# Token records of 132 words instead of 258, and the residual row formed again from them on ScalarE

## What is computed

```python
x = x + tanh(g_xattn) * attention(layernorm(x), ctx, ctx)       # 16 heads of 8
x = x + tanh(g_ffn) * moe(layernorm(x))

# moe: T = 4096 tokens, E = 8 experts, capacity C = T / E = 512
gates = softmax(tokens @ Wg); idx = argmax(gates)
place = position of the token among those of its expert (in order); dropped if place >= C
out = gate * (relu(token @ W1[idx] + b1[idx]) @ W2[idx] + b2[idx])    # 0 if dropped
```

## Time and profile before

| | us |
|---|---|
| median of 3 runs | 298.25 |
| lowest and highest | 296.54 and 298.52 |
| profiled execution, its own time | 298.6 |
| its span in the profile | 296.5 |
| attention stage in that span | 0 to some 218 |
| experts' stage | some 218 to the end |

### The profile page before, as it was taken

One profiled execution on the slowest core, in us unless ns is written; L12 is line 12 of the kernel. 1 busy time (PEld: TensorE's weight loads), 2 busy tenths in 40 slices (PEclk: granted clock), 3 DMA queues, 4 the chain that ended last, 5 costly groups with the idle time before them and its releaser, 6 DMA issues.

```text
span 296.5 us, 8184 instructions
## 1 busy us (share of the span) xinstructions
PE 244.5 (82%) x2907; PEld 163.5 (55%) x2907; DVE 196.6 (66%) x663; ACT 155.6 (52%) x375; POOL 182.3 (61%) x246
## 2 busy tenths in 40 slices
PE   1748758788979989999899989995869999999950
PEld 1325525465755755765656666663324677777740
DVE  4676717647978999989897999965302545555440
ACT  5553727567778787787887756681202322222100
POOL 6625916911982998897897968448720056555781
PEclk9998959969999999999999999999595999999995
DMA  4652771990482652661733541138352256554310
GB/s 120 184 162 73 214 217 32 237 293 19 113 235 57 174 158 71 195 182 46 213 110 90 152 126 57 58 102 174 138 144 66 71 170 188 173 180 132 103 55 16
DMA packets 50920, 39.27 MB, mean 132 GB/s; under 512 B 9698, under 2 KB 47223, under 8 KB 50880
## 3 DMA queue, kind: packets, MB, share of 16 engines
q1 hardware_dynamic: 47168, 28.67, 35.9%
q0 software_dynamic: 3712, 10.07, 10.4%
HBM read 13.72 MB, written 12.65 MB: 89 GB/s over the span
## 4 chain that ended last, share of the span: by engine, by line
PE 39%; DVE 13%; DMA 13%; SPq 10%; issue 9%; ACT 8%; POOL 4%; POOLq 0%; ACTq 0%; DVEq 0%
PE X L634 9%; DMA qp<-mrow 8%; DVE negm L833 6%; SPq L347 6%; PE TS L618 5%; PE M L546 3%; ACT prob L703 3%; PE O L513 3%; PE TS L497 3%; PE O L618 3%; PE M L618 2%; PE S L482 2%; PE X L441 2%; SPq L358 2%; POOL rec_dram L1224 2%
## 5 line engine op out<-in xcount | busy, mean ns | idle before, releaser
L703 ACT ACTIVATE prob<-TS 128x512 f32<-128x512 f32 x128 | 72.0, 589 | 40.1 <-PE TS L497 39.2
L833 DVE TENSOR_REDUCE negm<-S 128x4 f32<-128x512 f32 x128 | 81.6, 679 | 8.5 <-PE S L482 7.9
L513 PE MATMUL O<-prob,vals 128*32 128x128 f32 x1024 | 42.1, 283 | 0.8 <-ACT oraw L712 0.8
L1313 POOL DMA_INDIRECT out_dram<-fin,tok x32 | 31.5, 986 | 14.2 <-issue 12.2
L1224 POOL DMA_INDIRECT rec_dram<-rec,slot x32 | 32.2, 1005 | 8.0 <-issue 5.5
L497 PE MATMUL TS<-qp,kp 64*128 64x128 bf16 x512 | 28.1, 221 | 9.7 <-DMA qp<-mrow 9.6
L482 PE MATMUL S<-kp,qp 62*128 62x128 bf16 x512 | 31.3, 222 | 2.3 <-DVE negm L833 2.0
L513 PEld LDWEIGHTS O<-prob,vals 128*32 128x32 f32 x1024 | 24.6, 110 | 13.9 <-ACT prob L703 7.0
L267 POOL TENSOR_TENSOR rest_k<-full_k,parts_k 128x512 f32<-128x512 f32 x7 | 8.0, 1149 | 39.3 <-ACT parts_k L674 39.3
L804 ACT ACTIVATE qp<-TS,b_act 128x512 f32<-128x512 f32 x16 | 11.0, 687 | 39.9 <-PE TS L618 39.9
L634 PE MATMUL X<-w2s,qp 128*128 128x128 f32 x240 | 28.2, 275 | 0.9 <-issue 0.9
(11 more groups left out here) (170 smaller groups left out, 486.8 us busy)
## 6 DMA issues: line engine op xcount, KB each, us to landing
kp<-parts_k SPq DMA_DIRECT2D x48, 128.0 KB, 2.5
qp<-parts_q SPq DMA_DIRECT2D x48, 128.0 KB, 4.1
rec_dram<-zeros POOLq DMA_DIRECT2D x8, 516.0 KB, 6.2
xr<-rec_dram SPq DMA_DIRECT2D x8, 260.0 KB, 3.9
x_sb<-in_x_dram SPq DMA_DIRECT2D x8, 256.0 KB, 3.6
c_sb<-in_ctx_dram SPq DMA_DIRECT2D x8, 256.0 KB, 3.5
out_dram<-rec SPq DMA_DIRECT2D x8, 256.0 KB, 3.3
w1s<-in_L_ffn_W_dram SPq DMA_DIRECT2D x8, 256.0 KB, 4.1
```

The lines of the kernel that those rows point to most:

```text
L513: mm = nc.tensor.matmul(o_out[i * HV:(i + 1) * HV, u * L:(u + 1) * L], vals[G % 2][:, k, h, :], prob[n % 2][:, h * L:(h + 1) * L], start=( ...
L703: nc.scalar.activation(prob[n % 2][:, first:first + 4 * L], TS[:, a, :], ACT.Exp).then_inc(a_exp, 1)
L833: V.tensor_reduce(negm[n % 2][:, first:first + 4], S[:, a, :].rearrange("p (h k) -> p h k", k=L), AX.X, ALU.max, negate=True).then_inc(v_r ...
L1313: G_.indirect_dma_start(out_rows, bass.IndirectOffsetOnAxis(tok[p][:, t:t + 1], 0), fin[p][:, t, :], None, bounds_check=T - 1, oob_is_err= ...
```

## The change

A record now has 132 words: gate, code, mean, deviation sqrt(var + eps), and the normalised row. The row x itself is no longer in it. In SBUF `rec` holds, for each token, x (0 to 127), the eight logits, mean, deviation and the normalised row; gate and code overwrite the last two logits when these have been used, so that a record is one piece of 132 words. In the experts' stage ScalarE forms x again as normalised * deviation + mean, straight into `fin` (`rows_again`), and VectorE adds gate * b2 in place. The rows of expert e-1 are formed in ScalarE's part for expert e. `xr` and its DMAs are gone; `xe`, `gate2`, `tok` and `fin` have three buffers. One small GpSimd operation a group (`deviation`) is new, and `residual2` of the last expert stands earlier. The fill with zeros and the scatters of records keep their number and place; they carry 132 words a record.

```diff
-REC = 2 * P + 2
+REC = P + 4
...
+    GATE, CODE, MEAN, DEV, NORMED = DE - 2, DE - 1, DE, DE + 1, DE + 2
...
-        rec = [sb(f"rec{i}", [P, GB, D + DE]) for i in range(3)]
+        rec = [sb(f"rec{i}", [P, GB, NORMED + D]) for i in range(3)]
...
             def load_xe(e):
 
-                sp.dma_start(xe[e % 2][:], rec_v[e][:, :, 0:D]).then_inc(xe_in[e % 2], 16)
-
-            def load_xr(e):
-
-                sp.dma_start(xr[e % 2][:], rec_v[e][:, :, D:REC]).then_inc(xr_in[e % 2], 16)
+                sp.dma_start(xe[e % 3][:], rec_v[e]).then_inc(xe_in[e % 3], 16)
...
-            for e in range(2):
+            for e in range(3):
                 load_xe(e)
-            for e in range(2):
-                load_xr(e)
-            sp.wait_ge(p_eT, 1)
-            load_xe(2)
 
             for e in range(2, E):
                 sp.wait_ge(p_H, 4 * (e - 1))
                 load_w1(e)
                 if e < E - 1:
-                    sp.wait_ge(p_eT, e)
+                    sp.wait_ge(p_eT, e - 1)
+                    sp.wait_ge(v_code, e - 1)
+                    sp.wait_ge(a_res, e - 1)
                     load_xe(e + 1)
                 sp.wait_ge(p_Y, 2 * (e - 1))
                 load_w2(e)
-                sp.wait_ge(v_res, e - 1)
-                load_xr(e)
...
+            def rows_again(e):
+
+                act.wait_ge(xe_in[e % 3], 16 * (e // 3) + 16)
+                if e >= 3:
+                    act.wait_ge(fin_out[e % 3], 64 * (e // 3))
+                for t in range(ET):
+                    mm = nc.scalar.activation(fin[e % 3][:, t, :], xe[e % 3][:, t, 4:], ACT.Identity,
+                                              bias=xe[e % 3][:, t, 2:3], scale=xe[e % 3][:, t, 3:4])
+                mm.then_inc(a_res, 1)
...
                 nc.scalar.activation(xeT[p][:], S[:, p, :], ACT.Copy).then_inc(a_eT, 1)
+                if e >= 1:
+                    rows_again(e - 1)
+                if e == E - 1:
+                    rows_again(e)
...
             def residual2(e):
 
-                p = e % 2
-                dve.wait_ge(xr_in[p], 16 * (e // 2) + 16)
-                if e >= 2:
-                    dve.wait_ge(fin_out[p], 64 * (e // 2))
...
+                p = e % 3
+                dve.wait_ge(xe_in[p], 16 * (e // 3) + 16)
+                if e >= 3:
+                    dve.wait_ge(fin_out[p], 64 * (e // 3))
...
                 dve.wait_ge(v_gate2, e + 1)
+                dve.wait_ge(a_res, e + 1)
                 for t in range(ET):
                     mm = V.scalar_tensor_tensor(fin[p][:, t, :], b2_all[:, e, :], gate2[p][:, t:t + 1],
-                                                xr[p][:, t, 0:D], ALU.mult, ALU.add)
+                                                fin[p][:, t, :], ALU.mult, ALU.add)
...
             finish(E - 2, 0)
+            residual2(E - 1)
             finish(E - 2, 1)
             relus(E - 1)
-            residual2(E - 1)
...
+            def deviation(G):
+
+                pool.wait_ge(g_rs2, G + 1)
+                G_.tensor_tensor(rec[G % 3][:, :, DEV], rs2[:, 0, :], rs2[:, 1, :], ALU.mult).then_inc(g_dev, 1)
...
                 scaled(G)
+                deviation(G)
...
-                G_.indirect_dma_start(rec_dram, bass.IndirectOffsetOnAxis(slot[p][:, k:k + 1], 0), rec[p][:, k, 0:REC], None,
+                G_.indirect_dma_start(rec_dram, bass.IndirectOffsetOnAxis(slot[p][:, k:k + 1], 0), rec[p][:, k, GATE:], None,
                                       bounds_check=T - 1, oob_is_err=False).then_inc(sent[p], 16)
...
-                    root(NG - 1, mv2, rs2, v_mv2, g_e2).then_inc(g_rs2, 1)
+                    root(NG - 1, rec[(NG - 1) % 3][:, :, DEV], rs2, v_mv2, g_e2).then_inc(g_rs2, 1)
+                    deviation(NG - 1)
                     scatter(NG - 2, 3)
```

More of the change, by code:

```diff
@@ L161, in flamingo_kernel @@
         b1_dve = [sb(f"b1_dve{i}", [P, 1, FC]) for i in range(2)]
-        xe = [sb(f"xe{i}", [P, ET, D]) for i in range(2)]
-        xr = [sb(f"xr{i}", [P, ET, REC - D]) for i in range(2)]
+        xe = [sb(f"xe{i}", [P, ET, REC]) for i in range(3)]
         xeT = [sb(f"xeT{i}", [P, CAP]) for i in range(2)]
@@ L166, in flamingo_kernel @@
                for i in range(2)]
-        gate2 = [sb(f"gate2_{i}", [P, ET]) for i in range(2)]
-        tok = [sb(f"tok{i}", [P, ET], U32) for i in range(2)]
-        fin = [sb(f"fin{i}", [P, ET, D]) for i in range(2)]
+        gate2 = [sb(f"gate2_{i}", [P, ET]) for i in range(3)]
+        tok = [sb(f"tok{i}", [P, ET], U32) for i in range(3)]
+        fin = [sb(f"fin{i}", [P, ET, D]) for i in range(3)]
         s_cst, s_wqkv, s_bias, s_late = sem("s_cst"), sem("s_wqkv"), sem("s_bias"), sem("s_late")
@@ L202, in flamingo_kernel @@
         q_rest, k_rest = sem("q_rest"), sem("k_rest")
-        w1_in, w2_in, xe_in, xr_in, fin_out = sem2("w1_in"), sem2("w2_in"), sem2("xe_in"), sem2("xr_in"), sem2("fin_out")
+        w1_in, w2_in = sem2("w1_in"), sem2("w2_in")
+        xe_in, fin_out = [sem(f"xe_in{i}") for i in range(3)], [sem(f"fin_out{i}") for i in range(3)]
+        a_res, v_code, g_dev = sem("a_res"), sem("v_code"), sem("g_dev")
         b12_in, v_b1 = sem("b12_in"), sem("v_b1")
         p_eT, p_H, p_Y = sem("p_eT"), sem("p_H"), sem("p_Y")
-        a_eT, a_H, v_H, v_gate2, v_tok, v_res, v_fin = (sem("a_eT"), sem("a_H"), sem("v_H"), sem("v_gate2"), sem("v_tok"),
+        a_eT, a_H, v_H, v_gate2, v_res, v_fin = (sem("a_eT"), sem("a_H"), sem("v_H"), sem("v_gate2"),
                                                         sem("v_res"), sem("v_fin"))
@@ L412, in _ @@
                 load_w2(e)
-                sp.wait_ge(v_res, e - 1)
-                load_xr(e)
             for p in range(3):
                 sp.wait_ge(x1_out[p], 16 * len(range(p, NG, 3)))
-            for p in range(2):
-                sp.wait_ge(fin_out[p], 16 * ET * (E // 2))
+            for p in range(3):
+                sp.wait_ge(fin_out[p], 16 * ET * len(range(p, E, 3)))
         @block.tensor
@@ L602, in turn @@
             def turn(e):
-                pe.wait_ge(xe_in[e % 2], 16 * (e // 2) + 16)
+                pe.wait_ge(xe_in[e % 3], 16 * (e // 3) + 16)
                 if e >= 2:
@@ L875, in moments2 @@
                 for k in range(GB):
-                    mm = V.bn_aggr(mv2[:, k, :], st2[:, k, :])
+                    mm = V.bn_aggr(rec[G % 3][:, k, MEAN:DEV + 1], st2[:, k, :])
                 mm.then_inc(v_mv2, 1)
@@ L910, in done @@
                     dve.wait_ge(v_route, ROUTE * G + i)
-                lgs = rec[G % 3][:, :, 2 * D:2 * D + E]
+                lgs = rec[G % 3][:, :, D:DE]
                 dve.wait_ge(v_x1, GB * G + GB)
@@ L1168, in fence, with root @@
                 return G_.tensor_tensor(fence_p[:], pool_c[:, 0, 0:1], pool_c[:, 0, 0:1], ALU.add).then_inc(g_fence, 1)
-            def root(H, mv, rs, ready, e):
+            def root(H, var, rs, ready, e):
                 pool.wait_ge(ready, H + 1)
-                G_.tensor_tensor(rs[:, 0, :], mv[:, :, 1], pool_c[:, 0, :], ALU.add).then_inc(e, 1)
+                G_.tensor_tensor(rs[:, 0, :], var, pool_c[:, 0, :], ALU.add).then_inc(e, 1)
                 pool.wait_ge(e, H + 1)
@@ L1293, in _ @@
             pool.wait_ge(a_code, 1)
+            pool.wait_ge(g_dev, NG)
             pool.wait_ge(g_fence, NG - 1)
@@ L1305, in rows_out @@
                 if h == 0:
-                    pool.wait_ge(v_tok, e + 1)
+                    pool.wait_ge(v_code, e + 1)
                     pool.wait_ge(g_fence, NG + e)
```

36 lines of the change are left out of this document (18 added, 18 removed).

## The result

The changed kernel takes 289.17 us, the median of 4 runs (287.29 to 289.43). Beside it on the same chip the kernel before took 298.38 us (4 runs, 296.54 to 300.43). The ratio is 0.9704, with a 95% interval of 0.9654 to 0.9754: 3.0% faster, where 1.5% was predicted and the range ended at 290.0. Some runs of a kernel fall into a slower state of the chip; every ratio here leaves them out, while a median is that of all runs, so a ratio is not always the quotient of the medians beside it. The profiled execution of the changed kernel took 289.07 us, with a span of 287.3 us; before, the span was 296.5. The 9.2 us between these two spans are what has to be found.

A forecast was written before the change was run, and what follows sets the result against it. No engine is full everywhere; TensorE standing still for three slow `mrow` DMAs beside zero fills was taken as the bound. 298.6 - 1.3 - 1.9 - 1.7 + 0.4 = 294.1, less 0.35 gives 293.7 us; range 290.0 to 297.0.

The forecast's parts named there:

- The `mrow` DMAs wait for their own queue: Rival: early attention's `mrow` DMAs wait behind packing and an `x_sb` load, so about half the gain or less, 296.5 us; chance 0.26.
- the first wait: TensorE's wait for `mrow` at 35.73 us in early attention: smaller fills were to save 1.3 us, between 0.9 and 1.8.
- The other two waits: TensorE's waits for `mrow` at 53.57 and 60.81 us: smaller fills were to save 1.9 and 1.7 us.
- The page's rule: For the fills: a GpSimd DMA costs some 2.0 us plus bytes at 436 GB/s, so the three waits save 3.0 us.
- The deviation: One new 128x4 GpSimd operation in each of eight attention groups: taken to cost 0.4 us, from 0 to 1.75.
- the feared delay of the packing: In seven `norm2`, the added operation delays the query split, SyncE's packing and the next `mrow` DMAs: 0 to 1.75 us.
- smaller scatters and loads: At the change from attention to experts, fewer bytes in scatters and loads: between -0.2 and +0.2 us, taken as 0.
- ScalarE's rows: In the experts' stage, four more ScalarE operations an expert, some 1.65 us, fit in 3.84 us of idleness: nothing lost.
- the new wait on VectorE: In the experts' stage, `residual2` waits for ScalarE's rows: a gain for VectorE, none for TensorE, taken as 0.
- the tail: At the end, GpSimd's run of twelve scatters from 274.09 us sets the finish, so earlier `residual2(7)` brings 0.
- The clock at the first expert: Rival: TensorE's fall to half clock in expert 0 does not come, saving 3.4 us, to 290.3 us; chance 0.13.
- ScalarE's rows hold the experts: Rival: row operations above 0.96 us each delay relus and TensorE in six experts; 300.7 us at 1.25 each; chance 0.04.

## Why the prediction was right and where it was wrong

**The place and the mechanism were right.** The gain was put on the three `mrow` DMAs beside the zero fills, and there lies 7.7 of the 9.2 us. The run with full fills and the run with moved fills show that it is the fills and not the queue. That refutes the rival *The `mrow` DMAs wait for their own queue*, to which 0.26 had gone. One reading was loose: the two fills at 52.95 us do not both stand ahead of the second `mrow`. GpSimd issued them until 54.45, SyncE the two `mrow` DMAs at 52.98 and 53.57, so a fill beside the small DMA, and not only one ahead of it, goes with a slow landing.

**The step that failed is the size of the first wait.** The prediction took 1.3 us, between "half the bytes mean half the excess" and two fills' bytes at the stretch's rate. Batch 0 to 2 shrank from 11.89 to 8.81 us, by 3.1, and TensorE's wait from 3.90 to 0.89, by 3.0. Two things in the working were false. The floor was taken as 2.77 us from a row at 106.81, but `mrow` landed in 2.13 here and in 1.81 with the fills moved away. With that floor the excess was 1.79 us, while the landing alone became 2.43 shorter. And the excess did not halve with the bytes: against 1.81 it was 2.75 us and became 0.32. That holds for this pair of profiles; in the kernel with more rows on ScalarE the same DMA took 3.46 us beside the same small fills. The other 0.4 us of the wait came from SyncE, which issued this `mrow` 0.44 us earlier.

**The other two waits** had 1.9 and 1.7 us. Batch 3 to 5 gave 2.2 and batch 5 to 6 gave 2.4. Each passes its estimate, and the upper bounds of 2.0 and 1.7. In batch 3 to 5 that is the wait of 2.01, which went whole. In batch 5 to 6 the wait gave only 0.4 (1.21 to 0.79) and the other 2.0 are a term that the sum left out: TensorE had stood still for 2.01 and 1.21 us and did its work at a clock of 0.73, and without the first of these waits at 1.00. Together the three had 4.9 us with bounds up to 5.5; they brought 7.7.

**The page's rule** on GpSimd DMAs was rightly set aside: the fill's landing fell by 2.2 us (6.2 to 4.0; over all profiles with the fills at their old place that have this median, 5.3 and 6.2 against 4.0 to 4.3), where the rows of before gave 2.1 and 2.0 us plus bytes at 436 GB/s gives 0.6 (the Trainium skill, page "DMA: Bandwidth & Descriptors", section "Anatomy of one DMA — SWDGE (gpsimd) path").

**The deviation had the wrong sign**: +0.4 us was taken, with nothing below 0 as a bound; a row for a gain, the `mask` write of 1.05 us, was in the trace of before, but was not looked for. It brought 0.85 by luck of place, and the feared delay of the packing did not come: batch 6 to 27, with five more such operations, became shorter.

**Right as they stood**: smaller scatters and loads 0 (at most about 0.6 us between batches 6 and 27, where the kernel before with one small operation took 107.36, less than the changed one), ScalarE's rows 0, the new wait on VectorE 0, the tail 0. The stage from expert 2 on differs by 0.04 us, where 0.5 was allowed.

**The clock at the first expert** still falls, and that rival had the right time for a wrong reason. It brought 0.3 us. On the chain of the changed kernel TensorE is still at half clock in expert 0 and back within it:

```profile
216.01 1.71 PE O L611 x2
217.71 1.35 PE TS L611 x2
...
229.61 0.86 PE O L611 x2
```

Where the clock did count was between batch 5 and 6.

**ScalarE's rows hold the experts** was refuted, with its price. It had each expert pay what its ScalarE work exceeds 3.84 us by; tripled work exceeded it by 1 us and cost nothing in the inner experts. TensorE has another expert's output products to do before it needs the relu. The threshold of 1.15 us an operation, from which that case was to become slower than before, loses its ground with it.

So the sum's 4.5 us were 4.7 short of the span's 9.2: 2.8 in the three waits, 1.25 in the deviation (0.4 lost was taken, 0.85 gained was measured), and 0.65 in attention's later groups and the clock at the experts, less what batches 28 to 31 gave back.

## What to carry to other kernels

A large transfer that nobody waits for can be the dearest one in the kernel, if small ones that everybody waits for are issued behind or beside it: look for a DMA of a few KB that takes twice as long in one stage as in another, and at what was issued around it. As an upper bound, price the whole wait and not a share of the bytes, and add what TensorE loses by its clock after the wait: here that was 2.0 of 7.7 us. Moving such a transfer away in time is worth as much of a trial as shrinking it. And before a small operation on GpSimd is called a cost or free, look which two-input operation of VectorE it comes to stand beside.

## What the runs showed of the hardware that was not expected

- A `mrow` DMA of 4 KB took 1.81 and 1.84 us with the fills moved away, 2.13 to 3.59 beside fills of 264 KB, 4.39 to 5.44 beside 390 KB and 3.95 to 6.19 beside 516 KB, as far as it lies on the chain that ended last. Next to the moved bursts of 516 KB it took 4.32 to 4.70. Whether this goes with the bytes or has a knee is open.
- TensorE's same work from batch 5 to 6 took 6.88 us at a granted clock of 0.73, behind waits of 2.01 and 1.21 us, and 4.60 us at 1.00 without the first of them. A wait can cost as much again in the clock.
- A low clock ahead of a wait costs little. With 0.50 from 30 to 38 us in place of 0.93, the kernel before with one small operation took 11.06 us from batch 0 to 2 in place of 11.89: TensorE worked longer and waited 1.82 us in place of 3.90.
- Issuing DMAs takes SyncE longer while large fills run. Four packing DMAs in one line from about 36 us on took it 4.53, 4.05 and 3.45 us with fills of 516 KB, 3.02 with 390, 2.53 to 2.98 with 264 and 2.51 to 2.52 with the fills moved away. Why is not shown.
- A VectorE operation of 128x32 took 1.05 us instead of 0.20 when it started just behind a GpSimd operation of 128x512 of 1.04 us, and ended with it; shown by shifting GpSimd's operation by 0.2 us in two kernels. The Trainium skill, page "GPSIMD Engine Reference", section "1. Specifications", says that GpSimd and VectorE share their SBUF interfaces, with contention for VectorE instructions that have two SBUF inputs. The `mask` write has two, and the traces agree; no run varied the number of inputs.
- Kernels that are the same up to there took 5.15 to 6.96 us from batch 2 to 3 with fills of 264 KB at their old place: 5.15 at a granted clock of 1.00 from 38 to 46 us, 6.96 at 0.65. What decides the clock there stays open.
